# Token statistics of a layer norm moved from VectorE to GpSimd in the first attention stage of an eight-layer kernel

## The reference

```
def _layernorm(x, axis=-1, eps=1e-05):
    m = mean(x); v = var(x)                # over the 128 features
    return (x - m) / sqrt(v + eps)
x = x + L0_xattn_ref(_layernorm(x), ctx, Wq, Wkv, Wo)                # layer 0
x = x + L0_ffn_ref(_layernorm(x), norm_g, norm_b, slot_g, slot_b, scale, slot_embeds, ...)   # layer 1
```

## Time and profile before

| | us |
|---|---|
| median of 3 runs | 912.84 (912.43 to 914.34) |
| the profiled execution's own time | 912.43 |
| its span | 910.7 |
| TensorE busy | 870.1 |
| VectorE busy | 692.5 |
| ScalarE busy | 534.4 |
| GpSimd busy | 586.7 |

### The profile page before, as it was taken

How to read it: one execution, slowest core, us unless ns; L and a number is a source line. 1 busy time by engine, 2 the same in 40 slices (tenths; PEclk the granted TensorE clock), 3 DMA queues, 4 the chain that set the end, 5 groups by cost and what they waited for, 6 DMA issues and landing times.

```text
span 910.7 us, 16072 instructions
## 1 busy us (share of the span) xinstructions
PE 870.1 (96%) x4762; PEld 669.5 (74%) x4762; DVE 692.5 (76%) x1582; ACT 534.4 (59%) x1024; POOL 586.7 (64%) x580
## 2 busy tenths in 40 slices
PE   7998999999999899999999999999999998998997
PEld 5556676666697756888888888888888665775775
DVE  6998767899556788866666666666668778888886
ACT  3555667666743166666666666666666674445465
POOL 5933444788613145877777777777777777888620
PEclk9999999999999879999999999999999999999999
DMA  7000000322000000200000000000002000000001
GB/s 205 2 2 2 0 2 12 96 72 74 13 2 30 1 9 7 73 24 24 23 26 26 20 26 23 26 26 20 24 26 104 1 1 1 1 1 0 1 12 36
DMA packets 27432, 24.46 MB, mean 27 GB/s; under 512 B 3483, under 2 KB 24179, under 8 KB 27251
## 3 DMA queue, kind: packets, MB, share of 16 engines
q1 hardware_dynamic: 27379, 23.80, 8.8%
HBM read 22.74 MB, written 1.05 MB: 26 GB/s over the span
## 4 chain that ended last, share of the span: by engine, by line
PE 72%; DVE 15%; ACT 6%; POOL 5%; issue 2%; DVEq 0%; ACTq 0%; POOLq 0%
PE psum L1997 67%; POOL hh L759 3%; DVE arena L1550 2%; DVE arena L1547 2%; PE psum L2165 2%; DVE arena L1906 1%; ACT hh L889 1%; ACT arena L951 1%; DVE stats L1424 1%; PE psum L2242 1%; PE psum L2027 1%; ACT arena L889 1%; DVE arena L1799 1%; DVE mv L1427 1%; DVE arena L1556 1%
## 5 line engine op out<-in xcount | busy, mean ns | idle before, releaser
L1997 PE MATMUL psum<-xw 128*128 128x512 f32 x1248 | 322.8, 394 | 1.7 <-DVE arena L1799 1.0
L722 POOL TENSOR_TENSOR hh<-arena,hh 128x512 fp32r<-128x512 f32 x176 | 228.4, 1298 | 81.4 <-ACT hh L889 80.1
L1997 PEld LDWEIGHTS psum<-xw 128*128 128x128 f32 x1248 | 232.1, 188 | 54.2 <-issue 3.8
L1806 DVE TENSOR_TENSOR psum<-psum,arena 128x512 f32<-128x512 f32 x176 | 123.1, 699 | 97.7 <-PE psum L1997 91.4
L1143 ACT ACTIVATE arena<-psum 128x512 f32<-128x512 f32 x176 | 105.6, 600 | 120.2 <-PE psum L1997 120.1
L889 ACT ACTIVATE hh<-arena 128x512 fp32r<-128x512 f32 x228 | 142.2, 625 | 38.2 <-DVE arena L1906 34.6
L1997 PE MATMUL psum<-hh,wdn 128*128 128x512 f32 x528 | 148.3, 390 | 0.2 <-POOL hh L722 0.2
L1811 DVE TENSOR_TENSOR arena<-psum,arena 128x512 f32<-128x512 f32 x176 | 121.7, 692 | 7.7 <-DVE psum L1806 1.7
L1997 PEld LDWEIGHTS psum<-hh,wdn 128*128 128x128 f32 x528 | 98.9, 188 | 21.1 <-POOL hh L722 0.5
L1997 PE MATMUL psum<-arena 128*32 128x128 f32 (+6 forms) x992 | 85.6, 303 | 4.8 <-ACT arena L889 3.7
L889 ACT ACTIVATE arena<-psum 128x512 f32<-128x512 f32 (+6 forms) x85 | 57.5, 688 | 44.7 <-PE psum L1997 20.3
(11 more groups left out here) (299 smaller groups left out, 1493.0 us busy)
## 6 DMA issues: line engine op xcount, KB each, us to landing
egu<-in_w SPq DMA_DIRECT2D x44, 128.0 KB, 2.0
egu<-in_egu SPq DMA_DIRECT2D x16, 256.0 KB, 2.6
edn<-in_w SPq DMA_DIRECT2D x44, 64.0 KB, 1.8
edn<-in_edn SPq DMA_DIRECT2D x16, 128.0 KB, 2.1
arena<-in_w SPq DMA_DIRECT2D x1, 1536.0 KB, 6.4
X<-in_x SPq DMA_DIRECT2D x4, 256.0 KB, 4.0
arena<-in_ctxTd SPq DMA_DIRECT2D x2, 512.0 KB, 5.7
arena<-in_conv SPq DMA_DIRECT2D x1, 768.0 KB, 4.6
```

Of the source, the lines that this page charges most:

```text
L722: pool.tensor_tensor(hh[:, s % 4, 1, :], h1[:, s % 2, :], hh[:, s % 4, 0, :].bitcast(F32), ALU.subtract).then_inc(hh_lo, 1)
L1806: dve.tensor_tensor(bank(2 + k), bank(2 + k), sil[:, k, :], ALU.mult).then_inc(prod_done, 1)
L1997: return pe.matmul(dst, lhsT=lhsT, rhs=rhs, start=start, stop=stop)
```

## The change

Statistics, power and application of five groups, the groups 2 and 3 of layer 0 and 0, 1 and 2 of layer 1, become one function on GpSimd, `token_norm`. VectorE has no statistics for them any more. It sums by halving as the slots' norm does, over X and over the squared differences, with the slots' scratch. `ln_var` now counts only the groups that VectorE does, and `variances` gives the number to wait for. GpSimd's order is changed: the keys 1 to 3 first, then `token_norm` in turn with the other keys, then the slots' norm, then `token_norm(1, 1)` and `token_norm(1, 2)`. The scale and bias of the slots (`slot_gs`) are formed by VectorE in t = 5 and count in `se_n`, for which ScalarE and TensorE now wait at 2. In a `grouped` tile ScalarE copies the weights of t-1 ahead of the exponential of t, as in the other tiles.

```diff
+        STATS_BY_POOL = ((0, 2), (0, 3), (1, 0), (1, 1), (1, 2))
+        def variances(L, g):
+            return NG * L + g + 1 - sum(own <= (L, g) for own in STATS_BY_POOL)
...
-                pool.wait_ge(ln_var, NG * L + g + 1)
+                pool.wait_ge(ln_var, variances(L, g))
...
+                    def sums(half, rows):
+                        then(pool.tensor_tensor(half, rows[:, :, 0:D // 2], rows[:, :, D // 2:D], ALU.add))
+                        n = D // 4
+                        while n:
+                            then(pool.tensor_tensor(half[:, :, 0:n], half[:, :, 0:n], half[:, :, n:2 * n], ALU.add))
+                            n //= 2
+                    def token_norm(L, g):
+                        s, half, sq = slice(4 * g, 4 * g + 4), slot_half[:, 0:4, :], slot_sq[:, 0:4, :]
+                        if L == 0:
+                            pool.wait_ge(x_in[g], 16)
+                        else:
+                            pool.wait_ge(x_done, 4 * g + 4)
+                        sums(half, X[:, s, :])
+                        then(pool.tensor_scalar(mv[:, s, 0], half[:, :, 0], 1.0 / D, None, ALU.mult))
+                        if L == 1:
+                            pool.wait_ge(ln_tp, g + 1)
+                        then(pool.tensor_tensor(xn[:, s, :], X[:, s, :], wide(mv[:, s, 0:1], 4, D), ALU.subtract))
+                        then(pool.tensor_tensor(sq, xn[:, s, :], xn[:, s, :], ALU.mult))
+                        sums(half, sq)
+                        if L == 0:
+                            then(pool.tensor_scalar(veps[:, s], half[:, :, 0], 1.0 / D, EPS, ALU.mult, ALU.add))
+                        else:
+                            then(pool.tensor_scalar(veps[:, s], half[:, :, 0], (1.0 + EPS) / D, EPS * EPS, ALU.mult, ALU.add))
+                        pool.tensor_tensor(rstd[:, s], veps[:, s], neghalf[:, s], ALU.pow).then_inc(ln_rstd, 1)
+                        pool.wait_ge(ln_rstd, NG * L + g + 1)
+                        pool.tensor_tensor(xn[:, s, :], xn[:, s, :], wide(rstd[:, s].unsqueeze(2), 4, D), ALU.mult).then_inc(ln_xn, 1)
...
                     pool.wait_ge(krep_done, 1)
-                    keys(1)
-                    ln_power(0, 2)
-                    keys(2)
-                    keys(3)
-                    ln_power(0, 3)
-                    for b in range(4, B):
+                    for b in range(1, 4):
                         keys(b)
+                    token_norm(0, 2)
+                    keys(4)
+                    token_norm(0, 3)
+                    keys(5)
+                    token_norm(1, 0)
+                    keys(6)
+                    keys(7)
...
-                    then(pool.tensor_scalar(slot_gs[:, :], cols[:, COL["slot_g"]:COL["slot_g"] + 2], scal[:, 0:1], None, ALU.mult))
                     slot_sums(slot_raw)
...
+                    token_norm(1, 1)
+                    token_norm(1, 2)
                     continue
                 for g in range(NG):
-                    if L != 1 or g < NG - 1:
+                    if L != 1:
                         ln_power(L, g)
...   (ScalarE, loop of layer 0)
-                grouped = t % 4 == 2 and t < NT - 2
-                if 1 <= t <= NT and not grouped:
+                if 1 <= t <= NT:
                     weight_rows(t - 1)
...
-                if grouped:
-                    weight_rows(t - 1)
                 if t == NT:
-                    act.wait_ge(se_n, 1)
+                    act.wait_ge(se_n, 2)
...   (VectorE, loop of layer 0)
-                if t in (0, 2):
-                    ln_stats(0, 2 + t // 2)
+                if t == 5:
+                    dve.wait_ge(w_slots, 16 * N_SLOTS)
+                    dve.tensor_scalar(slot_gs[:, :], cols[:, COL["slot_g"]:COL["slot_g"] + 2], scal[:, 0:1], None, ALU.mult).then_inc(se_n, 1)
...
-                    if t in (6, 10, NT - 1):
-                        ln_stats(1, min(u // 4, 2))
+                    norm_behind(1, u)
...   (TensorE, t = 16)
-                    pe.wait_ge(se_n, 1)
+                    pe.wait_ge(se_n, 2)
```

More of the change, by code:

```diff
@@ L674, in ln_power @@
                         pool.wait_ge(ln_xn, NG * L + g)
-                    if L == 1:
-                        pool.wait_ge(ln_tp, g + 1)
                     then(pool.tensor_tensor(xn[:, s, :], X[:, s, :], wide(mv[:, s, 0:1], 4, D), ALU.subtract))
@@ L779, in quantised_norm @@
                     s = slice(4 * g, 4 * g + 4)
-                    pool.wait_ge(ln_var, NG * 7 + g + 1)
+                    pool.wait_ge(ln_var, variances(7, g))
                     then(pool.tensor_scalar(veps[:, s], mv[:, s, 1], EPS, None, ALU.add))
@@ L800, in keys, with slot_sums @@
                                            wide(rowmask[:, :].unsqueeze(2), H0 // 2, C), ALU.mult).then_inc(kbd_done[1], 1)
+                    def sums(half, rows):
[4 more added lines that the diff above has]
+                            n //= 2
+                    def slot_sums(rows):
+                        sums(slot_half, rows)
+                    def token_norm(L, g):
[18 more added lines that the diff above has]
+                        pool.tensor_tensor(xn[:, s, :], xn[:, s, :], wide(rstd[:, s].unsqueeze(2), 4, D), ALU.mult).then_inc(ln_xn, 1)
                     ln_power(0, 0)
@@ L804, in _ @@
                     pool.wait_ge(krep_done, 1)
-                    keys(1)
-                    ln_power(0, 2)
-                    keys(2)
-                    keys(3)
-                    ln_power(0, 3)
-                    for b in range(4, B):
-                        keys(b)
[L813 to L818, removed]
+                    for b in range(1, 4):
+                        keys(b)
+                    token_norm(0, 2)
[5 more added lines that the diff above has]
+                    keys(7)
                     pool.wait_ge(w_slots, 16 * N_SLOTS)
-                    then(pool.tensor_scalar(slot_gs[:, :], cols[:, COL["slot_g"]:COL["slot_g"] + 2], scal[:, 0:1], None, ALU.mult))
                     slot_sums(slot_raw)
```

## The result

The changed kernel takes 925.12 us (median of 4, 921.87 to 927.32) against 912.63 for the kernel before, ratio 1.0131 with a 95% interval of 1.0091 to 1.0172. Timed again later, once more beside the kernel before, it took 921.11 us (median of 12, 919.94 to 930.45) against 912.95, ratio 1.0099 (1.0069 to 1.0129). It is slower, by 8 to 12 us.

What follows compares the result with a forecast made beforehand. TensorE, busy 870.1 of 910.7 us, was taken as the bound, with VectorE full from 14 to 74 us. 912.43 + 8.0 (late dispatch) + 1.7 (clock) = 922.1, as a median 922.5 us; range 918.2 to 926.

Steps and rivals of the forecast that it cites:

- The queue sum: GpSimd's queue from 14.12 us: seven keys, the slots' norm of 16.20 us and five token norms of 10.88 end at 91.8 us.
- Without a gap: GpSimd would work from 14 to about 92 us without idle time, its inputs being there each time.
- The stall: TensorE waits at `ln_transpose(1, 2)` till 91.8 us instead of 83.29; the dispatches come 7.6 to 8.5 us later, taken as 8.0.
- the clock's term: After the wait ending at 91.8 us TensorE runs partly at its lower clock, losing 0.7 to 2.5 us, taken as 1.7.
- two stalls foreseen: TensorE idle twice for some 6 us, before 80.9 us at `ln_transpose(1, 1)` and before 91.8 us at `ln_transpose(1, 2)`.
- part 1: Layer 0's loop: VectorE loses five statistics blocks of 1.40 us, 7.0 us in all; the loop alone can gain 2.3 to 5.6 us.
- Rival A: The wait for GpSimd comes but TensorE's clock stays up: 920.8 us; chance 0.25.
- a microsecond either way: Other clock dips further on, about 296 and 762 us, may shift against the work by a microsecond either way.
- The order of ScalarE's queue: Exponential behind the copy in three grouped tiles: about 1 us each, 0 to 3 us, a cost only in the loop.
- Rival B: GpSimd, running without a pause beside VectorE, is 4% slower over 77 us: 3 us more, 925.5 us; chance 0.11.
- Rivals C and D: GpSimd in time, 907.2 to 910.5 us, chance 0.04; or loop gain and delay cancel, same within a microsecond, chance 0.03.

## Why the prediction was right, and where it was not

**The queue sum held.** Predicted 14.12 + 7.07 + 16.20 + 5 x 10.88 = 91.8 us, measured 91.19: the queue began 0.9 us earlier, a token norm took 10.83 in place of 10.88, and 0.55 us were idle.

**"Without a gap" did not.** `token_norm(1, 0)` had to wait for tile 3's addition, which I had put before 39 us and which came at 40.4 in the slower loop. This wait was 0.55 us in one profile of the changed kernel and 2.35 in the other. I had treated GpSimd's queue as independent of the loop, and through this one input it is not.

**The stall held.** The transpose came at 91.24 (91.8 predicted), the first dispatch at 93.86 (93.1 before the clock's term), the third at 97.83 (97.1 before the clock's term), 8.7 us late. Predicted for this place were 8.0 and 1.7, 9.7 us; the queue ended 0.6 us earlier than its sum, and the way from the transpose to the third dispatch was 4.95 us at the full clock, where I had 5.3.

**Of the two stalls foreseen only this one came.** The one at `ln_transpose(1, 1)`, before 80.9 us, rested on the loop's gain of part 1. Without the gain TensorE was itself there only at 79.97, when the second group's `xn` was all but ready (80.4). The prediction could lose this stall without harm, because the end of the queue sets the time whatever TensorE did before it.

**The clock's term held in size**, with some luck in its working: 1.7 us predicted, 1.64 found by filling the wait, 1.92 beside the other profile. I took 3.4 to 7 us at the lower level behind the stall, of which half is lost, less 1 us for waits of the restart. It was 3.5 us, and with nothing taken off half of it is 1.8; with my 1 us off it would have been 0.8. The mean clock of 0.72 over stall and restart, and 0.67 where the stall was 8.5 us, agree with the Trainium skill ("TensorE: Matmul & The Clock Gate", "Why this matters for your kernels"), which has the clock fall behind idle gaps. Rival A, the stall without the clock, has the granted clock and the 1.64 us against it; its 920.8 us alone could not be told from the 921.11 measured.

**What I had left to "a microsecond either way" was larger.** The clock's dips elsewhere, at 14 to 22 us and around 300 us, moved single executions by several us: the one around 300 alone by 3.2 us between the first two profiles. That is the likely source of the difference between 922.5 predicted and 925.12 measured first; the second measurement has 921.11. That the forecast lies between the two is in part luck.

**Part 1 failed.** I let the loop gain 2.3 to 5.6 us, on VectorE's full row and TensorE's idle 2.3 us. With the blocks left out it gained 0.4 us in all, some 1.4 without the early dip, and 0.53 us for each of the two blocks that can be read free of it. What the row did not show is where the blocks stood: in the grouped tiles TensorE itself has 5.05 us of work (33.64 to 38.69 in the kernel before, from one similarity product to the next), against VectorE's 3.78 for a tile. Of the 1.40 us of the block in t = 6, 0.17 stayed as the small operation, 0.69 became a wait for TensorE's product, and 0.53 were gained. Outside the grouped tiles VectorE's 3.78 remain, whatever is taken from the others.

**The order of ScalarE's queue** was rightly seen as a cost inside the loop of 0 to 3 us: 1.2 us alone, 2.35 with the blocks gone. The cover named for it, the stall, did cover it.

**Rival B** has no support: 128x512 takes 1.04 us at 19.50, with VectorE busy, and at 90.15, where VectorE was idle from 86.2 to 94.1 us. The contention that the Trainium skill names ("GPSIMD Engine Reference", "Key points") is with VectorE instructions in a two-port mode or with two SBUF inputs; the ones beside 19.50 read PSUM for their one or one of their two inputs, so this row doesn't test it. Rivals C and D asked for a token norm of 9.2 or 9.3 us; it never came near.

## What to carry to other kernels

When work moves to an engine that looks idle, write out that engine's whole queue with start and end of each entry, and hold every entry against the moment at which the consumer's queue comes to it, and against the moment at which its own inputs are there. The share of idle time doesn't show it: GpSimd was under half busy over 44 us and still ended 8 us late. And before counting on relief for a full engine, look tile by tile at whether the removed block stands where another engine is longer anyway; 1.40 us of removed work were worth 0.53.

## What the runs showed of the hardware

A stall can cost more than its length. After 5.95 us without work TensorE's same transposes took 1.12 instead of 0.60 us, and keeping it busy with products that nobody reads gave 1.64 us back. After a wait of 1.87 us, too, the granted clock was at its lower level (0.50 in 82 to 84 us of the kernel with ScalarE's order undone).

The spread of whole executions goes with the clock too: of one kernel's twelve, the fastest, with a mean clock of 0.985, and the slowest, at 0.968, lay 10.5 us apart; 35 executions of the kernel before ran from 911.50 to 921.09 us. So in a difference of a few microseconds the clock's dips in untouched stages must be read beside the stage that was changed. Comparing the start of one instruction in both traces, stage by stage, separates them: here 8.6 us of delay before 292 us, and 5.4 at 305.
